# First attention: the value products of a step cut into two halves of 256 columns and issued around the second pair of turned scores

## The reference, cut to what matters

```python
q, k, v = (proj(w_q), proj(w_k), proj(w_v))
scores = jnp.einsum('bhqd,bhkd->bhqk', q, k) / jnp.sqrt(jnp.float32(D_K))
attn = jax.nn.softmax(scores, axis=-1)
out = jnp.einsum('bhqk,bhkd->bhqd', attn, v)
```

## Time and profile before

| | |
|---|---|
| median of 3 runs | 3064.46 us (3059.49 to 3064.55) |
| profiled execution: span from first to last instruction | 3062.5 us |
| PE busy | 2417.9 us (79%) |
| DVE busy | 2037.0 us (67%) |
| ACT busy | 1590.3 us (52%) |
| granted clock of TensorE, mean | 0.880 |

### The profile page before, as it was taken

How to read it: one execution, slowest core, us unless ns; L and a number is a source line. 1 busy time by engine, 2 the same in 40 slices (tenths; PEclk the granted TensorE clock), 3 DMA queues, 4 the chain that set the end, 5 groups by cost and what they waited for, 6 DMA issues and landing times.

```text
span 3062.5 us, 36612 instructions
## 1 busy us (share of the span) xinstructions
PE 2417.9 (79%) x12216; PEld 1889.0 (62%) x12216; DVE 2037.0 (67%) x3145; ACT 1590.3 (52%) x3315; POOL 1155.5 (38%) x1016
## 2 busy tenths in 40 slices
PE   6986989768778866777889889998799998952058
PEld 4344347557667655766767678886578877842046
DVE  3834742578778457877853477885578785498884
ACT  1541640277666127766611166664276664699701
POOL 3011046142123521212356546665456764510071
PEclk9887899778889977888999999999899999965579
DMA  6123223020100120010022211111111111200011
GB/s 214 44 84 97 43 66 90 16 71 14 56 21 25 52 65 22 15 56 22 25 64 88 76 28 53 52 53 52 49 32 52 56 49 56 73 28 0 0 32 45
DMA packets 87842, 155.73 MB, mean 51 GB/s; under 512 B 8840, under 2 KB 17672, under 8 KB 87528
## 3 DMA queue, kind: packets, MB, share of 16 engines
q1 hardware_dynamic: 87656, 153.38, 16.9%
HBM read 138.21 MB, written 14.75 MB: 50 GB/s over the span
## 4 chain that ended last, share of the span: by engine, by line
PE 51%; ACT 15%; DVE 15%; issue 7%; POOL 3%; DVEq 0%; ACTq 0%; POOLq 0%
PE ps L651 45%; ACT tables L1343 5%; PE ps L665 5%; ACT m L1218 3%; DVE f_lo L1382 2%; DVE m_front L1503 1%; PE ps L790 1%; POOL w_lo L595 1%; ACT tables L1182 1%; ACT m L1192 1%; DVE f_hi L1381 1%; ACT L1218 1%; DVE loose L1485 1%; DVE stat L1397 1%; DVE m L1582 1%
## 5 line engine op out<-in xcount | busy, mean ns | idle before, releaser
L594 POOL TENSOR_SCALAR w_hi<-w_in 128x512 fp32r<-128x512 f32 x430 | 315.2, 733 | 1382.4 <-PE ps L651 802.9
L595 POOL TENSOR_TENSOR w_lo<-w_in,w_hi 128x512 fp32r<-128x512 f32 x430 | 624.7, 1453 | 35.9
L651 PE MATMUL ps<-m,tables 128*128 128x128 f32 x2048 | 301.4, 297 | 136.6 <-ACT tables L1182 135.4
L651 PE MATMUL ps<-hT_hi,w_lo 128*128 128x512 f32 x864 | 355.5, 411 | 28.5 <-DVE a L1427 11.7
L651 PEld LDWEIGHTS ps<-m,tables 128*128 128x128 f32 x2048 | 273.6, 209 | 156.0 <-issue 131.0
L651 PE MATMUL ps<-hT_hi,w_hi 128*128 128x512 f32 x864 | 342.6, 397 | 0.0
L651 PE MATMUL ps<-hT_lo,w_hi 128*128 128x512 f32 x864 | 342.2, 396 | 0.0
L1582 DVE TENSOR_TENSOR_SCAN m<-m,m 128x1028 f32<-128x1028 f32 x128 | 308.0, 2406 | 10.0 <-ACT m L1218 4.3
L1218 ACT ACTIVATE m<-m_rows,negA 128x256 f32<-128x256 f32 x512 | 217.3, 498 | 22.2 <-DVE m L1536 15.5
L1554 DVE TENSOR_TENSOR m<-m,m 128x1024 f32<-128x1024 f32 x128 | 177.6, 1388 | 55.3 <-PE ps L665 39.0
L665 PE MATMUL ps<-tables,m 128*128 128x128 f32 x1024 | 164.4, 292 | 63.1 <-DVE m L1582 39.7
(11 more groups left out here) (245 smaller groups left out, 5308.6 us busy)
## 6 DMA issues: line engine op xcount, KB each, us to landing
w_in<-units SPq DMA_DIRECT2D x430, 256.0 KB, 2.6
stack_scratch<-a SPq DMA_DIRECT2D x48, 256.0 KB
a<-stack_scratch SPq DMA_DIRECT2D x64, 192.0 KB, 4.4
m<-bc_scratch SPq DMA_DIRECT2D x16, 512.0 KB, 5.4
out<-x_sb SPq DMA_DIRECT2D x2, 1024.0 KB, 4.3
tables<-small SPq DMA_DIRECT2D x1, 1143.0 KB, 9.9
x_sb<-x SPq DMA_DIRECT2D x4, 256.0 KB, 3.6
x_sb<-x SPq DMA_DIRECT2D x1, 1024.0 KB, 7.6
```

The source lines that it names most:

```text
L594: c["did"](nc.gpsimd.tensor_scalar(w_hi[:, r], raw, 1.0, 1.0, ALU.mult, ALU.mult), s["unit_hi"])
L595: c["did"](nc.gpsimd.tensor_tensor(w_lo[:, r], raw, w_hi[:, r].bitcast(F32), ALU.subtract), s["unit_split"])
L651: ins = T.matmul(out, lhsT, rhs, start=start, stop=stop)
```

## The change

The value products of a step become two halves of 256 columns. The first half (four matmuls) is issued before the second pair of turned scores, the second half behind it. `a_values` is raised once a step as before, by the second half. The flag that starts an accumulation is set in the first half of a quad's first step alone.

```diff
+                def values(k, half):
+                    j, r = k // TT, k % TT
+                    if not 0 <= k < TT * A_QUADS:
+                        return
+                    if half == 0:
+                        need(s["a_exp"], 4)
+                        if r == 0:
+                            claim(6 + j % 2, s["a_quad_kept"])
+                    w = slice(half * HL, (half + 1) * HL)
+                    for h in range(4):
+                        ins = T.matmul(ps[h * A_VW:(h + 1) * A_VW, 6 + j % 2, w], a_v[:, r, (4 * j + h) * A_VW:(4 * j + h + 1) * A_VW],
+                                       a_pT[:, k % 2 * 4 + h, w], start=(r, half) == (0, 0), stop=(r, half) == (TT - 1, 1), tile_position=(0, h * A_VW))
+                    if half:
+                        ins.then_inc(s["a_values"], 1)
+
                 for k in range(TT * A_QUADS + A_LAG + 3):
                     scores_T(k - A_LAG, 0)
                     scores(k, 0)
                     scores(k, 1)
                     maxima(k)
+                    values(k - A_LAG - 1, 0)
                     scores_T(k - A_LAG, 1)
-                    kV = k - A_LAG - 1
-                    j, r = kV // TT, kV % TT
-                    if 0 <= kV < TT * A_QUADS:
-                        need(s["a_exp"], 4)
-                        if r == 0:
-                            claim(6 + j % 2, s["a_quad_kept"])
-                        for h in range(4):
-                            ins = T.matmul(ps[h * A_VW:(h + 1) * A_VW, 6 + j % 2], a_v[:, r, (4 * j + h) * A_VW:(4 * j + h + 1) * A_VW],
-                                           a_pT[:, kV % 2 * 4 + h], start=r == 0, stop=r == TT - 1, tile_position=(0, h * A_VW))
-                        ins.then_inc(s["a_values"], 1)
+                    values(k - A_LAG - 1, 1)
```

## The result

The change is slower: 3077.49 us median of 10 runs (3067.53 to 3095.10) against 3064.20 of 10 runs of the kernel before; ratio 1.0048, 95% interval 1.0025 to 1.0070. The forecast was 3061 us with a range from 3048 to 3074.

A forecast was written before the change was run, and what follows sets the result against it. The bound was a loop of turned scores, two exponentials, turned scores and value products, 3.15 us a pass. Terms of 0.2 + 0.2 - 1.7 - 0.8 - 1.7 = -3.8 us gave 3061 us, range 3048 to 3074.

The forecast's parts named there:

- The bound of a pass: Plain full-clock pass: a loop with slack before now closes, giving 3.21 us against 3.15, 0.06 longer.
- the loop through the second bank: From the first pair's second matmul, waiting for its bank, through second pair and exponentials back to that bank: 3.21 us.
- The price of a half: Value products of 256 columns take 0.58 us; two halves cost 1.16 instead of 1.00.
- The rival of a half that costs more: Each round of a half pays a fixed time; at 0.76 us a half, 0.2% slower; chance 0.13.
- Where a quad ends: Transposes mostly hidden but maxima late by 0.43 us: a quad 13.27 us against 13.25.
- passes 33 to 37: End of each batch row, without plain scores or maxima: full-clock passes 2.73 us against 3.15.
- The sum: All terms, 0.2 + 0.2 - 1.7 - 0.8 - 1.7, give -3.8 us, so 3061 us, 0.12% less.
- the six passes at the lower clock I put at nothing: Six passes at the lower clock taken to change by nothing, both loops being longer there alike.
- The rival of the clock: At the first row's end the clock may stay up: -4.3 us more, 3056 us; chance 0.25 together with cheap bounds.
- that falls or rises elsewhere: Sign against the prediction: a clock that falls or rises elsewhere in the two stages would make it wrong.
- a wait of 0.27 us: PE's wait for ACT between plain and turned scores, 0.27 us a pass, to be filled by the first half.

The follow-up runs named there:

- E2: Kernel before with whole value products of 512 columns moved ahead of the second pair, not cut: 3097.54 us, ratio 1.0097.
- E1: Kernel before with value products cut into two halves, both at the old place behind the second pair: 3062.03 us, ratio 0.9983.
- E4: The change in passes 32 to 38 alone, otherwise the kernel before: 3058.93 us, ratio 0.9975.
- G2: The kernel before, unedited, in one more profiled execution: span 3074.5 us, 96.8 us of the two rows low.
- G3: The change, unedited, in one more profiled execution: span 3059.5 us, 59.5 us of the two rows low.
- F1: The change in passes 7 to 15 alone, whole value products at the old place from pass 16 on: 3091.05 us, ratio 1.0056.
- E3: The change from pass 16 on, passes 7 to 15 as in the kernel before: 3063.27 us, ratio 0.9992.
- F4: E4 plus two unused matmuls behind each pair of plain scores in passes 0 to 6: 3058.89 us, ratio 0.9970 to the kernel before.

## Why the prediction was wrong

**The bound of a pass** was right: the loop through the second bank closes at 3.20 us (forecast 3.21), and E2, which lengthens what stands in that loop, lengthens the plain pass to the 3.61 us that its edges gave.

**The price of a half** was right: 0.57 us against 0.58, and it starts 0.32 us behind plain scores (152.97 to 153.29), taken as 0.34 without a row. The rival of a half that costs more is out; so is cutting as such (E1).

**Where a quad ends** was right in size, 13.21 us against 13.27, and so were **passes 33 to 37**, whose plain ones are 2.72 to 2.87 against 2.73; E4, which has them alone, takes 0.25% off (0.08% to 0.42%), part of which may be its clock (0.8811 against 0.8774).

**The sum** failed at one step: "the six passes at the lower clock I put at nothing". Most of these cost what they did, 4.61 us (5.66 where a quad ends), but their number was taken from one profile as if it were the kernel's own and would stay. In the first profile of the change it is nine and part of a tenth in each row, 98.0 us at the low level against 45.4. By the rows a pass of 4.61 us at the low level is one of about 3.2 at the full one, so 52.6 us more at the low level cost 52.6 x (1 - 3.2 / 4.61) = 16 us; with the forecast's -3.8 that is +12 against the 14.3 measured for the two stages of that execution. Another 1.1 us is from the first two low passes of each row (7 and 8), which are 4.81 to 4.94 us instead of 4.61. That this execution had so much more low time than the first profile of before is in part luck, as G2 and G3 show; that the change has more of it on average is shown by the mean clock of the runs.

**The rival of the clock** looked at the end of a row alone, and only at a gain. The clock there did stay up in the profile after; the loss came at the start of the rows, where the prediction named a clock "that falls or rises elsewhere" only among what would make it wrong, without a price or a chance.

Shown by timed runs: passes 7 to 15 alone bring a loss of this size (F1), which the change without them hasn't (E3); it isn't the cut (E1); and the lower mean clock is large enough for it. Not shown: by what the spreading in these passes holds the clock down. PE is about as busy in the low passes of both kernels (57.10 of 61.40 us in the change, 74.45 of 78.50 in G2), and F1's second row stayed low in passes with whole products.

## What to carry to other kernels

Follow a pass edge by edge around every loop that could close, not only the one that now does: filling a wait of 0.27 us moved it to another bank and gained nothing, as the sum said. Before trusting such a sum, count how much of the stage runs at TensorE's low level and read that from several executions, because here a fraction of a microsecond a pass was outweighed by some 1.4 us for each pass that ran low. And try an edit part by part: the part of this change without plain scores beside it is faster than both kernels (E4), while passes 7 to 15 alone lose as much as the whole change (F1).

## What was not expected of the hardware

In F4 PE was busy for 29.71 of 30.70 us and the level stayed at 0.50 all that time. The same kernel's low stretch at the start of a batch row differs widely between executions: 20.5 us in the first profile of before and 78.5 us in G2.
